# A cross-attention and FP4 feed-forward layer: a multiplication moved to GpSimd, a padded chunk, zeroing moved to VectorE, and the last output projection placed ahead of the second feed-forward row

## The reference

```python
x = x + xattn(layernorm(x), ctx, ctx, bias, mask)      # q, k, v projections, softmax(q k^T * SCALING + bias), output projection
x = x + ffn(layernorm(x))
def ffn(x):                                            # w_gate, w_up: 704 x 256, w_down: 256 x 704
    gate = fp4_linear(x, w_gate); y = fp4_linear(x, w_up)
    h = silu(gate) * y
    return fp4_linear(h, w_down)
def fp4_linear(x, w):                                  # both are quantized in blocks of 16 along the last dimension:
    ...                                                # scale = max|block| / 6, values rounded to 0, .5, 1, 1.5, 2, 3, 4, 6, times scale
```

## Time and profile before

| | us |
|---|---|
| median of 3 runs | 964.21 |
| lowest and highest run | 963.38, 964.72 |
| the profiled execution's own time | 963.4 |
| its span, first to last instruction | 961.6 |
| granted PE clock, mean over the span | 0.989 |
| busy: PE, DVE, ACT, POOL | 906.3, 733.7, 616.0, 477.7 |

### The profile page before, as it was taken

How to read it: one execution, slowest core, us unless ns; L and a number is a source line. 1 busy time by engine, 2 the same in 40 slices (tenths; PEclk the granted TensorE clock), 3 DMA queues, 4 the chain that set the end, 5 groups by cost and what they waited for, 6 DMA issues and landing times.

```text
span 961.6 us, 20204 instructions
## 1 busy us (share of the span) xinstructions
PE 906.3 (94%) x6740; PEld 707.7 (74%) x6740; DVE 733.7 (76%) x1879; ACT 616.0 (64%) x1148; POOL 477.7 (50%) x468
## 2 busy tenths in 40 slices
PE   5499999999999999999999999999779999999997
PEld 4376777777777777777777777777558888888785
DVE  5377666767766676676776688998479999999995
ACT  2277777777777776777777778778735555555542
POOL 5786876776786687677678557865000000000000
PEclk8799999999999999999999999999999999999999
DMA  5576633452442533345244253500000000000000
GB/s 169 144 225 146 137 101 91 102 133 63 112 120 61 131 90 100 94 102 132 62 111 122 61 135 102 138 13 1 1 1 12 23 18 16 16 16 16 16 16 28
DMA packets 50776, 76.45 MB, mean 80 GB/s; under 512 B 5248, under 2 KB 22016, under 8 KB 50688
## 3 DMA queue, kind: packets, MB, share of 16 engines
q1 hardware_dynamic: 50432, 75.06, 29.1%
q10 hardware_dynamic: 256, 0.26, 0.1%
HBM read 45.16 MB, written 29.36 MB: 77 GB/s over the span
## 4 chain that ended last, share of the span: by engine, by line
PE 85%; ACT 5%; issue 4%; DVE 3%; SPq 1%; DMA 1%; POOL 0%; ACTq 0%; DVEq 0%
PE psum L1183 27%; PE psum L1320 12%; PE psum L1274 12%; PE psum L1533 9%; PE psum L1205 5%; PE psum L1515 5%; PE psum L1517 4%; PE psum L1516 4%; PE psum L1238 3%; PE psum L1215 2%; ACT att L742 1%; ACT att L749 1%; SPq L386 1%; DVE att L917 1%; ACT att L688 1%
## 5 line engine op out<-in xcount | busy, mean ns | idle before, releaser
L1035 DVE CUSTOM_DVE_ANT_0 att<-psum,att 128x512 f32<-128x512 f32 x512 | 343.7, 687 | 175.6 <-PE psum L1274 174.5
L601 POOL TENSOR_TENSOR att<-att,neg_max 128x512 f32<-128x512 f32 x308 | 322.9, 1059 | 182.5 <-DVE neg_max L1035 179.7
L1183 PE MATMUL psum<-ident,att 128*128 128x128 f32 (+1 forms) x2576 | 381.7, 276 | 26.6 <-ACT att L742 12.1
L1183 PEld LDWEIGHTS psum<-ident,att 128*128 128x128 f32 (+1 forms) x2576 | 308.3, 141 | 100.8 <-ACT att L742 29.2
L742 ACT ACTIVATE att<-psum 128x512 f32<-128x512 f32 x512 | 298.9, 598 | 125.2 <-PE psum L1183 120.7
L1274 PE MATMUL psum<-stack 128*128 128x512 f32 x512 | 270.4, 529 | 14.3 <-DVE neg_max L1035 7.4
L749 ACT ACTIVATE att<-att,neg_max 128x512 f32<-128x512 f32 x204 | 147.0, 721 | 15.0 <-DVE neg_max L1035 14.8
L1274 PEld LDWEIGHTS psum<-stack 128*128 128x128 f32 x512 | 97.9, 191 | 49.1 <-issue 31.8
L1320 PE MATMUL psum<-att 128*32 128x256 f32 x2048 | 123.8, 382 | 0.0
L1533 PE MATMUL psum<-att 128*128 128x256 f32 (+1 forms) x384 | 97.9, 388 | 2.8 <-ACT att L866 2.8
L1320 PEld LDWEIGHTS psum<-att 128*32 128x32 f32 x2048 | 60.0, 109 | 44.6 <-issue 9.2
(11 more groups left out here) (98 smaller groups left out, 1007.4 us busy)
## 6 DMA issues: line engine op xcount, KB each, us to landing
stack<-qk_planes SPq DMA_DIRECT2D x124, 192.0 KB, 3.8
qk_planes<-k_hl SPq DMA_DIRECT2D x48, 256.0 KB
qk_planes<-q_hl SPq DMA_DIRECT2D x48, 256.0 KB
att<-in_fside_1xSxS_dram SPq DMA_DIRECT2D x32, 256.0 KB, 2.9
att<-in_ctx_dram SPq DMA_DIRECT2D x8, 512.0 KB, 6.7
out_dram<-att SPq DMA_DIRECT2D x32, 128.0 KB, 1.7
x<-in_x_dram SPq DMA_DIRECT2D x1, 3072.0 KB, 15.2
x<-in_x_dram SPq DMA_DIRECT2D x2, 512.0 KB, 5.8
```

Source lines behind the costliest of these rows:

```text
L601: pool.tensor_tensor(prob[:, slot, :], prob[:, slot, :], neg_max[:, slot:slot + 1].to_broadcast([P, S]), ALU.subtract).then_inc(less_pool, 1)
L1035: dve.tensor_tensor_reduce(out=prob[:, slot, :], in0=ps_score[:, SCORE_BANK[2 * S_ + r], :], in1=bias_m[:, tt, :], scale=-1.0, scalar=BIG, ...
L1183: return pe.transpose(out_, in_, ident[:, :])
```

## The change

The multiplication of L1164 goes from DVE to a new feed-forward step on POOL. `f_hq` gets 768 columns, of which POOL clears the last 64 once; transposes, the copy out of PSUM (now one instruction) and the down matmuls of the last chunk take all 128 rows. The clearing of slots 1 and 2 goes from POOL to DVE, behind `high_q(0)`. Octet 1's high and low parts are made three steps later in batch 0, two of batch 2's LayerNorm steps and `add_bo` one step later. The 3 MB DMA of x is cut in two: 512 KB where it was, 2.5 MB behind octet 1's stack. PE makes the last batch's output ahead of row 1's step.

```diff
-        f_hq = cut(2, I)
+        f_hq = cut(2, IC * P)
...
@@ SP
-            sp.wait_ge(stack_zero, 2)
+            sp.wait_ge(stack_zero2, 1)
             stack_quad(0, 1, 1)
...
-            sp.dma_start(x1[:, 2 * NT:ROWS, :], x_v[:, 2 * NT:ROWS, :]).then_inc(xrest_in, 16)
+            sp.dma_start(x1[:, 2 * NT:3 * NT, :], x_v[:, 2 * NT:3 * NT, :]).then_inc(x2_in, 16)
...
                 stack_octet(2 * b + 1)
+                if is_first(b):
+                    sp.dma_start(x1[:, 3 * NT:ROWS, :], x_v[:, 3 * NT:ROWS, :]).then_inc(xrest_in, 16)
@@ POOL
             rstd_of(0)
-            pool.memset(stack[:, 1:SLOTS, :, :, :].bitcast(F32), 0.0).then_inc(stack_zero, 1)
             pool.memset(vv, 0.0).then_inc(const_step, 1)
...
                     if S_ == 2 and first:
                         rstd_of(1)
+                    if S_ == 5 and first:
                         low_q(1)
-                    if S_ == (3 if first else 1):
+                    if S_ == (6 if first else 1):
                         low_k(2 * b + 1)
...
-                    if S_ == (18 if first else 10) and has_next2(b):
+                    if S_ == (19 if first else 10) and has_next2(b):
                         rstd_of(b + 2)
...
-                    if S_ in ((23, 25) if first else (19, 21)) and has_next2(b):
-                        add_bo(b + 2, S_ // 24 if first else S_ // 20)
+                    if S_ in ((24, 26) if first else (19, 21)) and has_next2(b):
+                        add_bo(b + 2, S_ // 26 if first else S_ // 20)
...
             rstd2_of(B - 1)
+            def step(n, par):
+                m = n - 2
+                if not live(m):
+                    return
+                pool.wait_ge(fhd_ready, m + 1)
+                if isinstance(m, int) and m == 0:
+                    pool.wait_ge(fgu_ready, 1)
+                    pool.memset(f_hq[:, :, I:IC * P], 0.0)
+                wait(pool, fhT_ready, m - 1)
+                pool.tensor_tensor(blocks(f_hq[:, par, 0:I]), blocks(f_hu), spread(f_s[:, 1 - par, 0:NHB], NHB),
+                                   ALU.mult).then_inc(fhq_ready, 1)
+            ffn_loop(pool, step)
@@ ACT
-                    act.activation(f_hqT[:, 1 - par, 0:IC - 1, :].rearrange("p c t -> p (c t)"), ps_h[:, 0:(IC - 1) * P], ACT.Copy)
-                    act.activation(f_hqT[0:ILAST, 1 - par, IC - 1, :], ps_h[0:ILAST, (IC - 1) * P:IC * P], ACT.Copy).then_inc(fhT_taken, 1)
+                    act.activation(f_hqT[:, 1 - par, :, :].rearrange("p c t -> p (c t)"), ps_h[:, 0:IC * P], ACT.Copy).then_inc(fhT_taken, 1)
@@ DVE
             high_q(0)
+            dve.memset(stack[:, 1:SLOTS, :, :, :].bitcast(F32), 0.0).then_inc(stack_zero2, 1)
...
-                    if S_ == 2 and first:
+                    if S_ == 5 and first:
                         dve.wait_ge(stacked[0], stacked_count(0))
                         high_q(1)
-                    if S_ == (3 if first else 1):
+                    if S_ == (6 if first else 1):
                         high_k(2 * b + 1)
...
-                        stats_at, apply_at = ((14, 15, 16, 17), (20, 21)) if first else ((5, 6, 7, 9), (14, 15))
-                        if first and S_ == stats_at[0]:
-                            dve.wait_ge(xrest_in, 16)
+                        stats_at, apply_at = ((15, 16, 17, 18), (21, 22)) if first else ((5, 6, 7, 9), (14, 15))
+                        if b < 2 and S_ == stats_at[0]:
+                            dve.wait_ge((x2_in, xrest_in)[b], 16)
...
-                if live(m2):
-                    dve.wait_ge(fhd_ready, m2 + 1)
-                    wait(dve, fhT_ready, m2 - 1)
-                    dve.tensor_tensor(blocks(f_hq[:, par, :]), blocks(f_hu), spread(f_s[:, 1 - par, 0:NHB], NHB),
-                                      ALU.mult).then_inc(fhq_ready, 1)
@@ PE
                     for c in range(IC):
-                        rows = P if c < IC - 1 else ILAST
-                        last = transposes(ps_h[0:rows, c * P:(c + 1) * P], f_hq[:, 1 - par, c * P:c * P + rows])
+                        last = transposes(ps_h[:, c * P:(c + 1) * P], f_hq[:, 1 - par, c * P:(c + 1) * P])
...
-                        rows = P if c < IC - 1 else ILAST
-                        last = pe.matmul(ps_y[:, 1 - par, :], f_hqT[0:rows, 1 - par, c, :], w_dnT[0:rows, c, :],
+                        last = pe.matmul(ps_y[:, 1 - par, :], f_hqT[:, 1 - par, c, :], w_dnT[:, c, :],
                                          start=c == 0, stop=c == IC - 1)
...
             make_oT(N_OCT - 1, 1, M0)
-            ffn_head(ffn_step, 1)
             pe.wait_ge(oT_taken, N_OCT)
             for i in range(2):
                 for piece in range(4):
                     make_out(i, piece, (M0, M1)[i])
-            ffn_loop(pe, ffn_step, 2)
+            ffn_loop(pe, ffn_step, 1)
```

More of the change, by code:

```diff
@@ L223, in xattn_ffn @@
         ps_y, ps_am = psum[:, 6, :].rearrange("p (i n) -> p i n", i=2), psum[:, 7, 0:NHB + NXB]
-        x0_in, xnext_in, xrest_in, w_in_sem, w_out_sem, ctx_in, mask_in, small_in = (
-            sem(n) for n in ("x0_in", "xnext_in", "xrest_in", "w_in", "w_out", "ctx_in", "mask_in", "small_in"))
+        x0_in, xnext_in, xrest_in, x2_in, w_in_sem, w_out_sem, ctx_in, mask_in, small_in = (
+            sem(n) for n in ("x0_in", "xnext_in", "xrest_in", "x2_in", "w_in", "w_out", "ctx_in", "mask_in", "small_in"))
         bias_in = [sem(f"bias_in{t}") for t in range(NT)]
@@ L247, in xattn_ffn @@
         stacked = [sem(f"stacked{i}") for i in range(SLOTS)]
-        stack_zero = sem("stack_zero")
+        stack_zero, stack_zero2 = sem("stack_zero"), sem("stack_zero2")
         q_plane, k_plane = sem("q_plane"), sem("k_plane")
@@ L377, in one, with blocks, spread @@
             return bass.ds(m, 1)
+        def blocks(a):
+            return a.rearrange("p (n k) -> p n k", k=BLOCK)
+        def spread(a, n):
+            return a.unsqueeze(2).to_broadcast([P, n, BLOCK])
         def first_rows(eng, qk, part, rows):
@@ L1092, in _ @@
             batches(dve, body)
-            def blocks(a):
-                return a.rearrange("p (n k) -> p n k", k=BLOCK)
-            def spread(a, n):
-                return a.unsqueeze(2).to_broadcast([P, n, BLOCK])
             def step(n, par):
```

## The result

| | before | after |
|---|---|---|
| median of 4 runs, us | 963.92 | 955.42 |
| lowest and highest run | 963.38, 964.72 | 954.42, 958.21 |
| ratio, 95% interval | | 0.9916, 0.9897 to 0.9935 |
| the profiled execution's own time | 963.4 | 958.2 |
| its span | 961.6 | 956.4 |

The kernel is 8.5 us faster by the medians. The profiled execution is the slowest of the four, 5.2 us shorter in span than the one of before. The prediction was 958.4. What follows first accounts for these 5.2 us; the other 3 are taken up with the head, in the part on the prediction. Single executions can fall into a slow state (one of the four of experiment 1 took 1501.97 us at a mean granted clock of 0.557), and these are left out of every comparison.

What follows compares the result with a forecast made beforehand. Three limits of a feed-forward row stood within hundredths: DVE's work 7.80, a dependency loop through PE, ScalarE and DVE 7.80, PE about 7.8. Terms -12.0 - 2.5 + 10.1 - 1.4 = -5.8 us gave 958.4 us, range 950 to 967.

Steps and rivals of the forecast that it cites:

- head, to batch 1: Start to batch 1: k's cast earlier, -7.6 us, and no wait on octet 0's planes, -4.4; together -12.0.
- passage, to the first full row: Attention to feed-forward: output matmuls ahead of row 1's gate bring the first full row 2.5 us earlier, 1.7 with low clock.
- 27 rows: Feed-forward: rows lengthen from 7.826 to 8.20 us with the product on POOL, +10.1 us over 27 steps.
- last rows: Last three feed-forward rows: padding the last chunk to 128 shows only there, -1.4 us, bounds 0 and -2.
- The exclusion: Feed-forward rows: POOL's product and DVE's two-SBUF-input instructions shut each other out, but for about 0.15 us on either side.
- Rival A: Feed-forward rows: POOL and DVE do not shut each other out, rows 7.80 us, total 946.8; chance 0.10.
- Rival B: Feed-forward rows: POOL's product costs 1.76 us, rows 8.54, total 967.9, slower from a price of 1.63; chance 0.16.
- The page rule: POOL's product at 2.6 cycles an element, 1.2 GHz: 1.53 us, row of 8.31, +13.1 us; not adopted.
- DVE has no gap in it: Feed-forward row before the change: DVE works without idle time through its 7.81 us.
- the ring: Feed-forward row: dependency loop through PE, ScalarE's x_abs, DVE's L1106 and L1111, back to PE's gate matmul; 7.80 us.
- so SP's queue holds: Batch 0: with the x load cut to 512 KB and 2.5 MB behind octet 1's stack, nothing queued on SP comes late.
- Rival C: Head: DVE's memset locks POOL out of low_q(0), first score at 27.1 to 30.2 us, total up to 962.6; chance 0.16.

Runs made afterwards that it cites:

- experiment 1: Changed kernel with the 704-column product back on DVE, padding kept: 950.52 us, ratio to the kernel before 0.9865.
- experiment 6: Changed kernel with the product cut to its first 16 columns and put on DVE (output differs): one execution, 949.95 us, rows 7.817.
- experiment 7: Changed kernel, product cut to 16 columns on DVE, and silu(gate) times up ahead of the rounding of x on DVE: one execution, 941.39 us, rows 7.413.
- experiment 10: Changed kernel with h and its maximum ahead of x's rounding, mask ahead of the 2.5 MB load, last chunk back at 64 rows: 946.5 us, rows 7.74.
- experiment 2: Changed kernel with batch 1's mask issued ahead of the 2.5 MB load of x: 953.2 us, ratio to the kernel before 0.989.
- experiment 11: Changed kernel with the last chunk of h back at 64 rows: 956.71 us, ratio to the kernel before 0.993, rows 8.007.
- experiment 3: Changed kernel with the last batch's output behind row 1 again on PE: 958.3 us, ratio to the kernel before 0.9947.
- experiment 5: Changed kernel with octet 1's high and low parts back at steps 2 and 3 of batch 0: 957.56 us, ratio to the kernel before 0.9933.
- experiment 8: Changed kernel with silu(gate) times up ahead of the rounding of x on DVE, product whole on POOL: 947.79 us, ratio to the kernel before 0.9846.
- experiment 9: Changed kernel with h and its block maximum ahead of x's rounding on DVE, and the mask ahead of the 2.5 MB load: 935.5 us, rows 7.41.

## Why the prediction was right, and where not

Times are from the profiled executions. The sum of the parts, predicted and measured against before:

| part | predicted | measured |
|---|---|---|
| head, to batch 1 | -12.0 | -7.1 |
| passage, to the first full row | -2.5 | -1.9 |
| 27 rows | +10.1 | +4.7 |
| last rows | -1.4 | -0.9 |
| sum | -5.8 | -5.2 |

Two terms are about 5 us off and cancel. The sign of each is as forecast, the total is right in part by luck.

**The exclusion** was the central step, and it holds as it was worked out: POOL in when L1179 ends, L1125's own work when POOL ends, 0.13 of overlap on one side and 0.15 on the other. Rival A (no exclusion, rows of 7.80) is refuted by L691's 1.97 in the median and by experiment 1. Rival B needed a price of 1.63 or more; it is 1.386 alone (the last of the 32, with DVE idle), within 0.04 of the 1.42 taken. The page rule (GPSIMD Engine Reference of the Trainium skill, Elementwise, side by side), which would have made the product 1.53 and the row 8.31, is 0.14 us too high for this form; the measurement decides.

**The mis-sized term is the row, 8.00 instead of 8.20, 5.4 us over 27 rows.** The step that failed is "DVE has no gap in it": I took the 6.20 us from L1106 to L1160 as DVE's own work. It held a wait:

```profile
827.94 0.42 DVE L1114 SCALAR_TENSOR_TENSOR att<-att 128x256 f32<-128x256 f32 x1
828.50 0.43 DVE L1117 TENSOR_REDUCE psum<-att 128x16 f32<-128x256 f32 x1
```

In this row of the kernel before (DVE in order of time), L1117 follows L1114 by 0.56, where in the row after (837.51 L1133, 837.84 L1136) it is 0.33. By the code it waits for ScalarE's L841, which ended at 828.47. Once POOL holds DVE back in each row, most of this wait is gone: from L1133 to L1136 it is 0.33 to 0.49, 0.39 in the mean. So the distance is 5.95 where none is left (836.37, where L1125 of 0.42 would have started, to 842.32) and 6.08 where 0.12 is (828.30 to 834.38), 6.01 in the mean, and 6.01 + 0.88 + 1.386 - 0.13 - 0.15 = 8.00. It also means that DVE alone was not at the limit before: its own work was about 7.6 (7.82 less 0.22), and the ring's 7.80 paced the rows. Experiments 6 and 7 show the ring directly, 7.82 with DVE idle 0.64 us a row, 7.41 once |x| is out of it. Of the three limits of the prediction the ring was the one that held; PE's own row, 7.74 by experiment 10, stood close below it, and DVE's 7.6 further.

**The head.** The chain came as worked out: apply over at 10.36 (10.2 said), PE at full clock, and 12.06 us from the cast to the first score (12.1). The cast came at 14.90 in this execution; 13.9 was said, and in the executions of experiments 2, 11 and 3 it came at 13.90, 13.93 and 14.01. The -4.4 for the wait on the planes is right too: 4.4 by experiment 5 against 2. By step 16 the head had given 11.2 of the 12.0, the cast being 1.0 us late. **The step that failed is "so SP's queue holds".** I followed what was behind the x load up to octet 1's stack and to rows 8 to 11 of x, and did not price the transfer right behind it, the mask. It took back 4.1 us in the profiled execution (step 16 to batch 1, 42.6 against 38.5), and less in others with the same head: the executions of experiments 3, 8, 1 and 11 waited 2.23, 2.25, 2.4 and 1.03 us for the mask and began batch 1 at 104.3, 104.8, 105.1 and 103.04. The last is 11.9 before the kernel of before, nearly the predicted 12.0. The spread of the changed kernel's runs, 3.8 us where before has 1.3, fits this varying wait, and so does that the median lies 2.8 us below the profiled execution; the other runs have no trace, so that is argued, not shown.

Rival C (DVE's clearing locks POOL's low parts out) did not happen: POOL's low_q ran first, and POOL's four L594 took 1.235 us each beside the clearing, no more than a two-input operation alone. The clearing was hidden, as said. This is also what the Trainium skill states (SBUF — State Buffer, Who interferes with whom) of a DVE instruction with at most one SBUF input outside the two-port modes; the trace agrees here, with a memset, in that L594 was not slowed. Whether POOL delayed the memset's start is open (last part).

**The passage.** The output first gives 1.9 us by the rows and 1.9 by experiment 3, against 2.5 forecast and 1.7 for the case with a low clock. It was the low clock: I had read that pauses of 3.2 us and more are followed by half clock and one of 1.69 is not, and let the 2.2 expected stand with the latter. The pause was 2.13, and from 701.9 on matmuls take 0.63 instead of 0.39.

**The padding** is worth nothing in the rows, as forecast (experiment 11), and 1.26 in the last rows (34.67 against 33.41). Against before only 0.9 of it is left; I put this down to the product on POOL, which comes later than it did on DVE, and did not test it. PE's own row is 7.41, not 7.2.

## What to carry to other kernels

Before moving work to GpSimd, look at what stands next to it on VectorE. Here operations with two SBUF inputs waited for the product, and a multiplication with one input in PSUM did not. The number of inputs is not the whole rule: POOL's clearing held a TENSOR_SCALAR with one tensor input. The product on POOL cost 4.6 us over 27 rows with L1125 next to it. In an order where h and its maximum stand there, which also takes |x| out of the ring, the row fell to 7.41. When an engine's row of work has no idle time in the profile, still compare each step's distance to its own length: a wait of 0.2 us hid between two short instructions. And of a large transfer that is moved in a queue, ask for the first small one behind it: 64 KB behind 2.5 MB took back 4.1 of the 11.2 us that the head had gained in the profiled execution.

## What the runs showed of the hardware that I had not expected

- A clearing on VectorE and one on GpSimd are about equally fast (6144 float32 a partition in 5.18 and 5.22 us), but they disturb differently: POOL's held DVE's TENSOR_SCALAR (7.29 for four instead of 2.14), DVE's left POOL's additions at 1.235 each. DVE's clearing began only at 18.22, 0.12 before POOL's low_q ended, after 1.23 us that nothing in the profile explains. The executions of experiments 1 to 3, 5 and 8 to 11 show the same 1.23, and 0.12 to 0.13 of overlap, much as at the other changes between POOL and DVE. Whether it waited for POOL was not tried.
- A weight load of 64 rows between loads of 128 shows a gap of 0.33 us on either side, yet padding it to 128 gains only 0.33 a row in all (7.74 to 7.41, experiments 10 and 9).
- PE's granted clock: after the pause of 2.13 us it fell from 1.00 to 0.50 for 3.4 us, one microsecond after the work had begun again. The pause of 1.69 in the kernel before had no such fall.
